# A transformer block with routed experts on one core: its list schedule searched over 600 trials, and the 24th block of each group left out

## The reference

```python
x = x + 0.5 * ffn(layernorm(x))      # layer 1
x = x + attention(layernorm(x))      # layer 2
x = x + 0.5 * ffn(layernorm(x))      # layer 3
```

## Time and profile before

| | us |
|---|---|
| runs shown | 593.38, 589.21, 592.57 |
| their median | 592.57 |
| profiled execution, its own time | 589.03 |
| profiled execution, its span in the trace | 587.2 |
| PE busy in it | 498.8 |
| gathers and the end behind the last matmul | about 32 |

### The profile page before, as it was taken

One profiled execution on the slowest core, in us unless ns is written; L12 is line 12 of the kernel. 1 busy time (PEld: TensorE's weight loads), 2 busy tenths in 40 slices (PEclk: granted clock), 3 DMA queues, 4 the chain that ended last, 5 costly groups with the idle time before them and its releaser, 6 DMA issues.

```text
span 587.2 us, 11232 instructions
## 1 busy us (share of the span) xinstructions
PE 498.8 (85%) x3136; PEld 412.5 (70%) x3136; DVE 353.1 (60%) x1059; ACT 286.1 (49%) x630; POOL 334.1 (57%) x338
## 2 busy tenths in 40 slices
PE   1745699999999999999999999999999889999600
PEld 0634588877787778877888788877787778787500
DVE  2674687735557776898558785697448733334311
ACT  4521655555573675536754466565542245555400
POOL 3337626565688588366875568836555553045072
PEclk9967699999999999999999999999999999999955
DMA  8931222542252211332113331153232253333212
GB/s 266 339 98 54 85 60 78 148 123 78 73 141 54 58 50 56 104 92 73 46 49 109 86 84 43 42 144 88 75 86 63 75 161 95 99 91 94 71 49 58
DMA packets 78090, 54.89 MB, mean 93 GB/s; under 512 B 9776, under 2 KB 72880, under 8 KB 78032
## 3 DMA queue, kind: packets, MB, share of 16 engines
q1 hardware_dynamic: 69840, 37.37, 22.2%
q0 software_dynamic: 8192, 16.79, 10.5%
HBM read 27.92 MB, written 26.21 MB: 92 GB/s over the span
## 4 chain that ended last, share of the span: by engine, by line
PE 75%; issue 8%; DVE 6%; POOL 4%; ACT 3%; DMA 2%; POOLq 0%; SPq 0%; DVEq 0%; ACTq 0%
PE gu L827 15%; PE gu L785 8%; PE ht_ps L818 8%; PE gu L787 7%; PE gu L786 7%; PE gu L745 4%; PE ht_ps L838 4%; PE gu L746 4%; PE gu L747 4%; PE xt_ps L768 3%; POOL x_sorted L1112 2%; PE misc L847 2%; PE misc L907 1%; POOL yg L1133 1%; DVE hs L1178 1%
## 5 line engine op out<-in xcount | busy, mean ns | idle before, releaser
L1133 POOL DMA_INDIRECT yg<-y_sorted,places x128 | 124.3, 971 | 127.5 <-PE gu L787 61.8
L1112 POOL DMA_INDIRECT x_sorted<-xn,places x128 | 127.4, 995 | 93.1 <-issue 30.3
L827 PEld LDWEIGHTS gu<-w,hT 128*128 128x128 f32 x768 | 95.4, 191 | 25.6 <-issue 21.7
L827 PE MATMUL gu<-w,hT 128*128 x768 | 105.9, 281 | 7.5 <-ACT hT L967 5.9
L962 ACT ACTIVATE gs<-gu 128x512 f32<-128x512 f32 x128 | 76.2, 596 | 65.7 <-PE gu L747 42.4
L785 PE MATMUL gu<-w,xbt_hi 128*128 x192 | 88.7, 462 | 3.5 <-DVE hs L1178 0.9
L1178 DVE TENSOR_TENSOR hs<-gs,gu 128x512 f32<-128x512 f32 x96 | 65.5, 684 | 32.7 <-ACT gs L962 29.5
L1165 DVE TENSOR_TENSOR xbt_lo<-xt_ps,xbt_hi 128x256 fp32r<-128x256 f32 x96 | 40.5, 421 | 73.0 <-ACT xbt_hi L952 72.4
L787 PE MATMUL gu<-w,xbt_hi 128*128 x192 | 76.0, 396 | 0.0
L786 PE MATMUL gu<-w,xbt_lo 128*128 x192 | 76.0, 396 | 0.0
L967 ACT ACTIVATE hT<-ht_ps 128x512 f32<-128x512 f32 x96 | 57.4, 598 | 32.9 <-PE ht_ps L818 31.2
(11 more groups left out here) (132 smaller groups left out, 845.4 us busy)
## 6 DMA issues: line engine op xcount, KB each, us to landing
xb<-x_sorted SPq DMA_DIRECT2D x96, 128.0 KB, 2.4
y_sorted<-ys SPq DMA_DIRECT2D x96, 128.0 KB
x_sorted<-yg SPq DMA_DIRECT2D x6, 512.0 KB, 6.2
X<-x_dram SPq DMA_DIRECT2D x8, 256.0 KB, 5.5
x_sorted<-xn,places POOLq DMA_INDIRECT x128, 2.3
yg<-y_sorted,places POOLq DMA_INDIRECT x128, 2.6
out_dram<-X SPq DMA_DIRECT2D x8, 256.0 KB
raw<-gate_w_dram SPq DMA_DIRECT2D x4, 256.0 KB, 5.1
```

The source lines that it names most:

```text
L827: mm = pe.matmul(dst[:, j * D:(j + 1) * D], hT[r % 2][:, at:at + P], w_flat[:, bass.ds(expert[r][j] + 2 * GU + half * D, D)], start=half = ...
L1112: nc.gpsimd.indirect_dma_start(x_sorted[l, g], bass.IndirectOffsetOnAxis(places[l, g][:, k, t:t + 1], 0), xn[:, b, t % T], None).then_inc( ...
L1133: nc.gpsimd.indirect_dma_start(yg[slot][:, k, t], None, y_sorted[l, g], bass.IndirectOffsetOnAxis(places[l, g][:, k, at:at + 1], 0)).then_ ...
```

## The change

`search` runs `schedule` 600 times. Each trial takes the shifts of urgency of the best plan so far, redraws those of 1, 3, 10 or 40 random families (a family is all operations of one name for one batch, pair or group; the shift is normal with deviation 1.2, or zero one time in five), and is kept if its plan is no longer than the best. The seed is fixed, so the plan is the same in every build. `schedule` may now fail, and then the trial is dropped. The planner's length for `regs` goes from 90 to 40. The last pair of every group holds one block: `width` is 1 there, and its front has only the half j = 0. The lengths of that pair's other operations in the plan stay those of two blocks.

```diff
+ROUNDS, SEED = 600, 1
...
+def width(l, g, n):
+
+    return min(2, blocks(l, g) - 2 * n)
...
-ROOM = max(2 * pairs(*lg) for lg in GROUP_LIST) * P
+ROOM = max(blocks(*lg) for lg in GROUP_LIST) * P
...
-        self.schedule()
+        self.search()
...
+    def unit(self, u, *needs, halves=2):
+        if halves == 2:
+            self.op(("front", u, 1), "PE", 70, *needs)
+            needs = (("front", u, 1),)
+        self.op(("front", u, 0), "PE", 70, *needs)
...
-            op(("regs", r), "PE", 90, ("table", l, g), ("front", ("R", r - 1), 0) if r >= 1 else None)
+            op(("regs", r), "PE", 40, ("table", l, g), ("front", ("R", r - 1), 0) if r >= 1 else None)
...
+    def family(self, key):
+
+        return (key[0], *key[1][0:3]) if key[0] in ("front", "silu", "hid") else key[0:3]
+
+    def search(self):
+
+
+        serial = {key: n for n, key in enumerate(self.ops)}
+        plain = {key: (self.urgency(key), self.stage(key), serial[key]) for key, o in self.ops.items() if o[0]}
+        family = {key: self.family(key) for key in plain}
+        families = sorted(set(family.values()), key=str)
+        rng = np.random.default_rng(SEED)
+        best, shift = None, {}
+        for n in range(ROUNDS):
+            trial = dict(shift)
+            if n:
+                for i in rng.integers(len(families), size=rng.choice((1, 3, 10, 40))):
+                    trial[families[i]] = rng.normal(0, 1.2) if rng.random() < 0.8 else 0
+            rank = {key: (u + trial.get(family[key], 0), *more) for key, (u, *more) in plain.items()}
+            if self.schedule(rank) and (best is None or max(self.end.values()) <= best[0]):
+                best, shift = (max(self.end.values()), rank), trial
+        self.schedule(best[1])
...
-                sp.dma_start(xb[r % XB][:], x_sorted[l, g][2 * n * P:2 * (n + 1) * P].rearrange("(j p) d -> p j d", p=P)
-                             ).then_inc(xb_loaded[r % XB], 16)
+                k = width(l, g, n)
+                sp.dma_start(xb[r % XB][:, 0:k], x_sorted[l, g][2 * n * P:(2 * n + k) * P].rearrange(
+                    "(j p) d -> p j d", p=P)).then_inc(xb_loaded[r % XB], 16)
...
-                for q in range(4):
+                for q in range(HALVES * width(*plan.pair[r])):
...
-                for j in range(2):
+                for j in range(width(*plan.pair[r])):
```

More of the change, by code:

```diff
@@ L216, in routed @@
         cut = [("cut_w_lo", e) for e in range(E)] if r == 0 else [("front", ("R", r - 1), 0)]
-        self.unit(u, ("pair_lo", r), ("regs", r - n % LOADED), *cut)
+        self.unit(u, ("pair_lo", r), ("regs", r - n % LOADED), *cut, halves=width(l, g, n))
         self.gated(u)
@@ L372, in dynamic @@
                 u, j = key[1], key[2]
-                if j == 1:
+                single = u[0] == "R" and width(*self.pair[u[1]]) == 1
+                if j == 1 or single:
                     if n and ("front", self.units[-1], 0) not in end:
@@ L408, in settle @@
             name = key[0]
-            if name == "front" and key[2] == 1:
+            if name == "front" and (key[2] == 1 or (*key[0:2], 1) not in ops):
                 self.units.append(key[1])
@@ L459, in schedule @@
                     best = (t, serial[key], key, engine, t)
-            assert best, ("no piece can begin", sorted(waiting, key=str)[:20])
+            if not best:
+                return False
             _, _, key, engine, t = best
@@ L478, in through @@
         t = self.start[key]
-        return tuple(sum(1 for u in self.units if self.end["front", u, j] + HOP <= t) for j in (1, 0))
+        return tuple(sum(1 for u in self.units if self.end.get(("front", u, j), t) + HOP <= t) for j in (1, 0))
 def build(nc, x, wq, wqp, wk, wv, wg, wo, lepe_w, lepe_b, sgate, sup, sdown, gate_w, up_w, down_w,
@@ L543, in build @@
         places = {lg: sb("places%d_%d" % lg, [P, 2, tiles(*lg)], I32) for lg in groups}
-        offsets = {lg: sb("offsets%d_%d" % lg, [P, 2 * pairs(*lg)], I32) for lg in groups}
+        offsets = {lg: sb("offsets%d_%d" % lg, [P, blocks(*lg)], I32) for lg in groups}
         TMAX = max(tiles(*lg) for lg in groups)
@@ L575, in build @@
         sorted_rows = [nc.dram_tensor(f"x_sorted{i}", [ROOM, D], F32).ap() for i in range(ROOMS)]
-        x_sorted = {lg: sorted_rows[i % ROOMS][0:2 * pairs(*lg) * P] for i, lg in enumerate(groups)}
-        y_sorted = {lg: nc.dram_tensor("y_sorted%d_%d" % lg, [2 * pairs(*lg) * P, D], F32).ap() for lg in groups}
+        x_sorted = {lg: sorted_rows[i % ROOMS][0:blocks(*lg) * P] for i, lg in enumerate(groups)}
+        y_sorted = {lg: nc.dram_tensor("y_sorted%d_%d" % lg, [blocks(*lg) * P, D], F32).ap() for lg in groups}
         x_loaded = [sem(f"x_loaded{b}") for b in range(B)]
@@ L779, in front @@
                     pe.wait_ge(xbt_lo_done, r + 1)
[L780 removed]
+                    if r == 0:
                         pe.wait_ge(w_lo_done, E)
@@ L1343, in table @@
             def table(l, g):
-                nb, at, s = 2 * pairs(l, g), g * PLACE_LINKS, place_link[l]
+                nb, at, s = blocks(l, g), g * PLACE_LINKS, place_link[l]
                 link(s, at + 4)
```

36 lines of the change are left out of this document (20 added, 16 removed).

## The result

The kernel after takes 574.52 us (median of 4 runs, 573.22 to 576.39), against 592.63 of the kernel before beside it (4 runs, 589.21 to 593.38). The ratio is 0.9708, with a 95% interval of 0.9658 to 0.9757: 18.1 us less, where 18.5 were forecast. The total was met. Its parts were not, as the experiments show: the blocks gave some 4.5 of their 12.5 us, the search nearly twice its 6, and in another place than predicted. In what follows, the medians and ratios leave out five executions in a slower state of the chip, one of e1's seven and four of e4's ten.

What follows compares the result with a forecast made beforehand. PE was taken as the bound, busy 460.04 of 480.00 us between 75 and 555 us. Blocks 12.5, regs price 0 and search 6 made 18.5 us off 592.6: 574.1, rounded to 574, range 562 to 585.

Steps and rivals of the forecast that it cites:

- The total: Whole kernel: 18.5 us off, from 592.6 to 574.1, rounded to 574; 568 to 577 given a chance of 0.47.
- The blocks: Eight 24th blocks without rows, one a group, left out: 12.5 us gained, between 11.3 and 13.6.
- the uncovered wait: A one-half front waits at once for earlier rows to be copied out: 0 to 0.7 us a group, taken as 0.
- The weight loads as a measure: PE load judged by weight loads, 80%: the pairs' halves would give 10.0 us; the prediction did not adopt it.
- Only the blocks (580): Rival: blocks give 12.5 us, the search's shorter plans give nothing on the chip; 580 us, chance 0.24.
- The price of regs: Planner's length for register reads before fronts, 90 to 40: worth 0, within 1 us either way.
- The search: Reordering fills PE's idle time: 6 us, 4 net from the head and 2 from later gaps; range -6 to 15.
- The head as the cheap fix of one family: First 62 us: one root ranked ahead of the scatters fills PE's 8.63 us wait, 4 us net.
- the head is filled: Rival: the search takes 15 us, with both holes of the first 62 us closed; 565 us, chance 0.17.
- The seventh group: Layer 3 gathers split its scatters and PE waits 2.4 us at its start; the plan may ease this.
- Slower (603), by holes at group starts: Rival: late loads stop PE's in-order queue at seven group starts, 22.7 us lost against 12.5; chance 0.04.
- The tail: Last 32 us, gathers on POOL with PE idle: unchanged within 1 us.

Runs made afterwards that it cites:

- e1: The kernel after with one plan (no search) and the old regs price of 90, so only the blocks left out: 586.57 us, ratio 0.9903 to before.
- e4: The kernel before with only the planner's length for regs at 40 instead of 90: 597.00 us, ratio 1.0078 to before.
- e2: The kernel after with one plan (no search), blocks left out and regs at 40: 588.31 us, ratio 0.9939 to before.
- e10: The kernel after with search seed 6 instead of 1, on another, slower chip: 615.25 us, ratio 0.9689 to before there.
- e5: Before's order of every engine held fixed, only the 24th block's instructions taken out: 586.08 us, ratio 0.9925 to before.
- e7: After with one plan and two rules: layer 3 gathers rank last, five layer 3 shared experts wait for the last routed front: 568.99 us, ratio 0.9633 to before.
- e8: e7 with one layer 1 root also ranked ahead of the first group's scatters: 573.48 us, ratio 0.9717 to before.
- e9: e7's two rules together with the search of 600 trials, seed 5, on the slower chip: 588.02 us, ratio 0.9258 to before there.
- e3: The kernel after, search and regs at 40 included, but with all 24 blocks computed as in before: 564.41 us, ratio 0.9551 to before.
- e11: The kernel after with search seed 4 instead of 1, on the slower chip: 620.59 us, ratio 0.9737 to before there.
- e6: After's order of every engine held fixed, with the 24th blocks computed as in before: 579.24 us, ratio 0.9799 to before.

## Why the prediction was right or wrong

**The total** is right: 574 forecast, 574.52 measured. It is right because two wrong terms cancelled, some 8 us too much for the blocks and 5 too little for the search, and that is luck. Measured apart, 4.5 and 11.3 us make 15.8, 2.3 short of the 18.1; intervals of some 3 us on each ratio leave room for that.

**The blocks** were mis-sized: 12.5 us, measured 4.5 (5.4 by the ratios in after's order). The spacing of 1.39 to 1.71 us a block is nearly right as work: busy time fell by 9.8 and 10.1 us, 11 had been written down. The step that failed is "whatever is taken off PE between 75 and 555 us counts nearly in full", and with it the choice of 0 between 0 and 0.7 us for the uncovered wait. With the order held fixed, 5.7 to 6.1 us of waits and stalls came up in its place, 0.7 to 0.8 a group. Of these some 2 us are longer waits for DVE, which fits the reading that a half front and its transposes are also the cover under which the other engines deliver for the next unit; at which units these waits stand was not followed. The named wait for the rows' copy is 1.1 us in one order and nothing in the other. The stalls without a semaphore, 3.7 and 2.5 us, are a term that the prediction did not have, and their cause stays open.

**The weight loads as a measure.** As the prediction applied the Trainium skill (Perfetto Trace Analysis, Identifying the Most-Contended Engine), with the share of weight loads as the measure of TensorE's load, the blocks would have been worth 80% of 12.5, 10.0 us, an estimate. Its direction was right, since a part did stay as idle time; its size was not. The measured share is 4.5 to 5.4 of 12.5, about 40%.

**Only the blocks (580)** as a rival priced them at 12.5 too. Alone they give 586 to 587.

**The price of regs** was taken at 0, and that holds for the sum; alone, e4 shows a loss of 0.8%. The reading beneath it was wrong. I took 24 idle times ahead of fronts for the 24 register reads the earlier trace rows. The same idle time of the weight load in e2 and in e10:

```profile
PEld gu L820 <- issue: 12.7, 29, 1.0
```

```profile
PEld gu L820 <- issue: 29.8, 39, 2.1
```

The number is 24 in before, 27 in after, 29 in e2, 23 in e5 and e7, 39 in e10. Yet the register reads are as many in each. That one count matched was chance, and "the new price is right where 90 was not" had no ground.

**The search** was mis-sized, and its place was wrong: 6 us expected, 4 of them from the head; 11.3 measured, none from the head. The head as the cheap fix of one family was refuted by e8, where one root among the scatters costs 4.5 us; whether the three more roots ahead of all scatters in e9 pay was not isolated. The rival "the head is filled" (565) did not happen in after.

**The seventh group** The earlier trace rows was seen, and priced at nothing but a risk. The search moved exactly those gathers behind the scatters.

**Slower (603), by holes at group starts**: after has none; PE is at 96% between 75 and 539.73 us, as forecast. The danger was real, though: in e1 PE waits 3.27 us for loaded rows ahead of the transposes at 507.77.

**The tail** of 32 us was forecast as unchanged, and is. What I missed is that it needn't be: I counted only the chain of gathers in it, and not that PE has 22 to 28 us of work with no need to be done before.

## What to carry to other kernels

Before you count removed work of the busiest engine in full, look at what becomes visible behind it: hold the order of instructions fixed, take out the work alone, and compare busy and idle time of the same stretch; here more than half came back as idle time. An idle stretch at the end of the busiest engine is worth more than its gaps: ask first which of its work depends on nothing there and can be moved into it. A planner's own length tells good orders from bad ones while the differences are large; below one or two per cent only runs decide.

## What the runs showed of the chip that I had not expected

Idle time of TensorE that no semaphore explains differed by program and by chip: none of PE in the kernels with 24 blocks (e3: 0.4 us), 1.5 to 4.9 us in those with 23. On the slower chip it was 11.7 to 14.0 us in all four kernels. A row of e11's timeline:

```profile
122.82 0.50 PE L780 MATMUL gu<-xt_hi,sw_hi 128*128 128x512 f32 x1 [2.43 <-issue]
```

It begins a shared expert's product, which waits for nothing that the trace shows, and is 2.43 us late. What sets these stalls stays open; the kernel before was not profiled on that chip, so what is the chip's and what the program's is not separated there.

The same 129 matmuls of the head took 26.94 to 28.94 us in different executions on the first chips. The timelines show two kinds of head. The first shared expert's matmuls begin at 16.61 us in before and at 16.17 in e6, in the same order, and go from 0.63 to 0.4 us each, the faster of the two clock levels, at 18.46 in the one and at 21.01 in the other:

```profile
18.46 0.44 PE L746 MATMUL gu<-xt_hi,sw_lo 128*128 128x512 f32 x1
```

```profile
21.01 0.45 PE L786 MATMUL gu<-xt_lo,sw_hi 128*128 128x512 f32 x1
```

The head of e6 then ends 1.1 us later (63.17 against 62.07). before, after, e1 and e8 were caught with the early kind, e2, e5, e6 and e7 with the late one. A difference of 1 us between two profiled spans can be this and nothing else.
